# The inverse norms of q and k in a windowed attention layer: Newton steps on GpSimd replaced by a logarithm and an exponential on ScalarE

## What is computed

```python
def l2norm(t):
    return t / jnp.maximum(jnp.linalg.norm(t, axis=-1, keepdims=True), 1e-12)
...
def attn_layer(x, Wqkv, qs, ksc, Wo):
    q, k, v = jnp.split(x @ Wqkv, 3, -1)          # 16 heads of 64
    ...
    q = l2norm(q) * qs
    k = l2norm(k) * ksc
    q = q * cos * scale + rotate_half(q) * sin * scale
    k = k * cos * inv + rotate_half(k) * sin * inv
    out = local_attention(q, k, v)                # windows of 32, softmax
    return out.transpose(0, 2, 1, 3).reshape(b, n, INNER) @ Wo
...
for i in range(6):
    x = attn_layer(shift_tokens(x), Wqkv[i], q_scale[i], k_scale[i], Wo[i]) + x
    x = ffn_layer(shift_tokens(x), ...) + x
```

## Time and profile before

| | |
|---|---|
| median of 3 runs | 5080.17 us (5074.98 to 5081.27) |
| profiled execution | span 5070.2 us from the first to the last instruction |
| PE matmul busy | 4363.6 us (86%) |
| PE weight load busy | 3053.5 us (60%) |
| DVE busy | 3369.4 us (66%) |
| ACT busy | 2462.3 us (49%) |
| POOL busy | 2562.9 us (51%) |
| mean granted clock of TensorE | 0.949 of full speed |

### The profile page before, as it was taken

One profiled execution on the slowest core, in us unless ns is written; L12 is line 12 of the kernel. 1 busy time (PEld: TensorE's weight loads), 2 busy tenths in 40 slices (PEclk: granted clock), 3 DMA queues, 4 the chain that ended last, 5 costly groups with the idle time before them and its releaser, 6 DMA issues. The chain is left out here.

```text
span 5070.2 us, 182187 instructions
## 1 busy us (share of the span) xinstructions
PE 4363.6 (86%) x69459; PEld 3053.5 (60%) x69459; DVE 3369.4 (66%) x7024; ACT 2462.3 (49%) x5161; POOL 2562.9 (51%) x4541
## 2 busy tenths in 40 slices
PE   8999956866899988998789988899888998799986
PEld 5777733654566655666566665666656666466663
DVE  3555533266777757777577775777757776677765
ACT  3555543222555535555355553555535555355542
POOL 0000000011787717877177872778627776278761
PEclk9999967988999999999999998999999999999998
DMA  1000001201222212222122221222212222122211
GB/s 37 5 4 4 2 1 40 70 7 41 71 65 68 57 30 66 65 65 57 37 61 65 67 53 39 65 65 65 50 39 65 65 65 50 45 61 66 65 47 34
DMA packets 453969, 243.92 MB, mean 48 GB/s; under 512 B 41158, under 2 KB 447892, under 8 KB 452116
## 3 DMA queue, kind: packets, MB, share of 16 engines
q1 hardware_dynamic: 453140, 232.66, 18.6%
HBM read 35.40 MB, written 4.19 MB: 8 GB/s over the span
## 5 line engine op out<-in xcount | busy, mean ns | idle before, releaser
L2453 DVE TENSOR_TENSOR n_tt<-n_pp,n_rot 128x1024 f32<-128x1024 f32 x768 | 922.4, 1221 | 528.9 <-ACT n_sq L2316 528.1
L1949 POOL TENSOR_TENSOR n_pre<-n_tt 128x512 f32<-128x512 f32 x768 | 961.2, 1275 | 233.1 <-DVE n_tt L2453 232.4
L2065 PE MATMUL n_pp<-n_wqkv,n_xT 128*128 128x512 f32 x1536 | 793.9, 619 | 11.1 <-ACT n_xT L2311 10.1
L1984 POOL TENSOR_TENSOR n_pre<-n_pre,n_rn 128x512 f32<-128x512 f32 x768 | 776.9, 1043 | 34.5 <-POOL n_rn L1972 34.5
L2316 ACT ACTIVATE n_sq<-n_pp 128x512 f32<-128x512 f32 x768 | 459.0, 598 | 594.0 <-PE n_pp L2065 583.4
L2081 PE MATMUL n_pp<-ident,n_pre 128*128 128x128 f32 x3072 | 452.8, 282 | 152.8 <-POOL n_pre L1984 152.6
L2328 ACT COPY n_qkT<-n_pp 128x512 f32<-128x512 f32 x768 | 437.3, 594 | 290.1 <-PE n_pp L2081 288.7
L2081 PEld LDWEIGHTS n_pp<-ident,n_pre 128*128 128x128 f32 x3072 | 366.3, 146 | 292.9 <-issue 287.8
L2460 DVE TENSOR_REDUCE n_ss<-n_sq 128x8 f32<-128x512 f32 x768 | 519.3, 676 | 0.0
L2095 PE MATMUL n_pp<-n_wo,n_OT 128*128 128x128 f32 x3072 | 403.4, 286 | 57.5 <-ACT n_OT L2334 57.5
L2095 PEld LDWEIGHTS n_pp<-n_wo,n_OT 128*128 128x128 f32 x3072 | 366.6, 196 | 102.1 <-ACT n_OT L2334 101.4
(11 more groups left out here) (263 smaller groups left out, 8187.8 us busy)
## 6 DMA issues: line engine op xcount, KB each, us to landing
n_V<-n_Vn SPq DMA_DIRECT2D x768, 128.0 KB, 2.6
n_Vx<-n_Vn SPq DMA_DIRECT2D x384, 128.0 KB, 2.5
n_Vx<-n_Vn SPq DMA_DIRECT2D x576, 64.0 KB, 2.2
n_wqkv<-in_L_ffn_Wqkv SPq DMA_DIRECT2D x6, 1536.0 KB, 6.8
e_w<-in_L_ffn_w SPq DMA_DIRECT2D x32, 256.0 KB, 3.0
m_Y<-e_ye SPq DMA_DIRECT2D x64, 64.0 KB, 2.0
n_wo<-in_L_ffn_Wo SPq DMA_DIRECT2D x6, 512.0 KB, 7.3
a_xs<-in_L_attn_x SPq DMA_DIRECT2D x16, 128.0 KB, 2.1
```

The costliest lines, as they stand in the source:

```text
L1949: nc.gpsimd.tensor_tensor(d, s[0], s[1][:, :, ::-1, :], ALU.add).then_inc(s_add, 1)
L1984: nc.gpsimd.tensor_tensor(d, d, bcast(rn[:, j, t, 8 * half:8 * half + 8], 2, D), ALU.mult).then_inc(s_kn, 1)
L2065: nc.tensor.matmul(pp[:, c % 2, :], xT[:, j * P:(j + 1) * P], wqkv[:, t * I + 512 * half:t * I + 512 * half + 512], start=True, stop=True) ...
L2453: nc.vector.tensor_tensor(tt[:, c % 4, :, :].rearrange("p s (h d) -> p s h d", d=D), bcast(pp[:, c % 2, :].rearrange("p (h d) -> p h d", d ...
```

## The change

GpSimd keeps the clamp of the sums of squares, now `clamp_squares`, and the products. A new function of ACT, `inverse_norms`, takes the natural logarithm of the clamped sums into a new tile `lg` and then the exponential of minus a half times it into `rn`. The products wait for `s_rn`, which ACT now raises. At the start of each layer ACT asks for the table set that has both functions. In the prologue of a layer ACT makes the pair ahead of the square of chunk 5; in the attention it makes it behind the first two squares of each half, for the second half of N at j = 0 and for the first half of N + 1 at j = 1.

```diff
-            def inverse_norms(N, j):
+            def clamp_squares(N, j):
 
                 x = ss[:, j, :, :].rearrange("p t h -> p (t h)")
-                y = rn[:, j, :, :].rearrange("p t h -> p (t h)")
-                steps = Steps(pool, s_nd, NORM_STEPS)
...
                 after(pool, s_ss, 8 * N + 4 * j + 4)
-                after(pool, s_kn, 8 * N - 4 + 4 * j)
                 held(pool, s_held)
-                link(nc.gpsimd.tensor_scalar(x, x, 1e-24, None, ALU.max))
...
+                nc.gpsimd.tensor_scalar(x, x, 1e-24, None, ALU.max).then_inc(s_clamp, 1)
 
             def norm(N, j, r):
                 t, half = 1 - r // 2, r % 2
+                after(pool, s_rn, 2 * N + j + 1)
                 after(pool, s_add, 8 * N + 4 * j + r + 1)
...
+            def inverse_norms(N, j):
+
+                after(act, s_clamp, 2 * N + j + 1)
+                nc.scalar.activation(lg[:, j, :, :], ss[:, j, :, :], ACT.Ln).then_inc(s_ln, 1)
+                after(act, s_kn, 8 * N - 4 + 4 * j)
+                after(act, s_ln, 2 * N + j + 1)
+                nc.scalar.activation(rn[:, j, :, :], lg[:, j, :, :], ACT.Exp, scale=-0.5).then_inc(s_rn, 1)
...
             def prologue(N, l):
+                nc.scalar.preload_act_table_set("natural_log_exp_and_others")
                 for kind, c in PROLOGUE:
                     bank = bank_of[kind, c]
+                    if (kind, c) == ("qk", 5):
+                        inverse_norms(N, 0)
...
                     if nxt:
                         square(N + 1, 4 * j)
                         square(N + 1, 4 * j + 1)
+                    if nxt or not j:
+                        inverse_norms(N + j, 1 - j)
+                    if nxt:
                         copy_v(N + 1, 1 - u, 2 * j, bank("v", 2 * j, 1), pairs[0] + u)
```

More of the change, by code:

```diff
@@ L1684, in l1_network @@
     TG = GR * NT
-    NORM_STEPS = 13
     ident, X, neghalf = env["ident"], env["X"], env["neghalf"]
@@ L1760, in l1_network @@
         rn = sb("rn", [P, NT, 2, H])
-        nt = sb("nt", [P, 2 * H])
+        lg = sb("lg", [P, NT, 2, H])
         pre = sb("pre", [P, NT, 2, I])
@@ L1806, in l1_network @@
         s_rn = sem("norms_made")
-        s_nd = sem("norm_steps")
+        s_clamp = sem("squares_clamped")
+        s_ln = sem("norms_logged")
         s_kn = sem("qk_normed")
@@ L1992, in prologue @@
                     add(N, c)
-                inverse_norms(N, 0)
+                clamp_squares(N, 0)
                 for r in range(4):
@@ L2003, in attention @@
                     stage(N + 2, u, b + 2)
-                inverse_norms(N, 1)
+                clamp_squares(N, 1)
                 for r in range(4):
@@ L2009, in attention @@
                         add(N + 1, c)
-                    inverse_norms(N + 1, 0)
+                    clamp_squares(N + 1, 0)
                     for r in range(4):
```

## The result

The changed kernel takes 4911.6 us (median of 4 runs, 4901.34 to 4916.32); the kernel before, run beside it on the same chip, takes 5077.7 us (4 runs, 5074.98 to 5081.27). The ratio is 0.9676, interval 0.9664 to 0.9688. The mechanism is as forecast and its size is not. What remains to be explained is why the gain is larger than the sum: the forecast added the printed waits of PE at five places of a layer, and those in its middle gave more than was printed.

A forecast was written before the change was run, and what follows sets the result against it. PE's waits for GpSimd's products with the inverse norm, 152.6 us, were taken as what the change could free. Five places gave 19.65 us a layer, 118 in six, plus 17 for the clock: 5080.2 - 135 = 4945 us, range 4918 to 4990.

The forecast's parts named there:

- the step from span to median: The 10.0 us between the profiled span of 5070.2 and the median of 5080.2 us, taken over as it stands.
- (d): Middle of a layer: all 8.9 us of PE's printed waits for the products go.
- (e): Last sequence of a layer: PE's wait of 1.8 us for the products goes.
- (a): Prologue of a layer: with a round trip of 1.06 us, PE's wait of 7.44 us shrinks by 4.65 to 2.8.
- (b): First sequence, first half: the exponentials are next late, so PE gains 2.9 us, not 4.67.
- (c): First sequence, second half: the exponentials are next late, so PE gains 1.4 us, not 2.59.
- (f): PE's granted clock behind the three long waits: 2.9 us a layer regained, 17 us in all.
- Only the edges gain: Rival, 10%: the middle's freed wait reappears at ACT's copies; only 54 us gained, 5026 us.
- ACT's queue becomes the bound: Rival, 4%: ACT stands at the logarithm, delaying everything behind it; at 3.5 us a call, 5264 us.
- The tables do not stay loaded: Rival, 2%: logarithm and exponential each fetch their own table in every call; 5215 us.

The follow-up runs named there:

- pad13: The changed kernel with thirteen dummy steps on GpSimd between clamp and products, making a call about as long as before; 5069.5 us, ratio 0.9991.
- pad7: The changed kernel with seven linked dummy steps on GpSimd between clamp and products; 4934.2 us, ratio 0.9714.
- newton2: The kernel before the change with two Newton steps instead of three; 4944.7 us, ratio 0.9752.
- `middle`: The change only in the sequences between the first and last of each layer, Newton steps on GpSimd elsewhere; 5003.0 us, ratio 0.9854.
- the repetition: The changed kernel run once more, unaltered, in a later call; 4915.5 us, ratio 0.9684 against the kernel before.
- `tables`: The changed kernel with a table load forced ahead of the logarithm and of the exponential in each call; 5120.7 us, ratio 1.0096.

## Why the prediction was right in its mechanism, and where its size was wrong

**The mechanism held.** GpSimd's calls are one clamp and a wait of 1.44 us (0.7 to 2 forecast), its busy time fell by 598 us (600), the wait for `n_pre` is 14.3 us (under 25), and the exponentials wait 2.17 and 0.79 us in the first sequence (2 and 1). The kernel pad13 shows that this call's length is all that the gain hangs on. The time came out 6.4 us below the range, and two steps of the sum put it there, the price of the waits in the middle and the step from span to median; with either of them right the time would have been inside.

**The middle (d): the term that was mis-sized.** "All 8.9 us" was right in kind: pad7 and newton2 get it back whole, `middle` alone gives 71.7 us. In size it was 12.45 us a layer, 21 us more in six. The step that failed was to take the printed idle time for the price of a wait. Behind the output projection each printed wait cost 0.16 us more, in all 114 waits of the middle, so that the waits alone are 11.77 us a layer where 8.9 were taken, 17 us more in six; the rest is within what two executions differ by. The last sequence (e) gave 2.39 us for 1.8, or 1.54 by the repetition: no difference that the runs can tell.

**The prologue (a): the trip was sized too long.** It is 0.67 us, not 1.06, since the three handovers cost 0.03, 0.09 and 0.09 us instead of 0.2 each; GpSimd's 0.18 was the wrong model for handovers that involve ScalarE. The wait that is left is 2.39 us for 2.8. Together with a part of the clock for which I had taken nothing, the place gave 5.55 us for 4.65.

**The first sequence (b), (c): right, in its sum by luck.** The exponentials are next late, as named. The waits fell from 4.67 to 2.17 and from 2.59 to 0.79, by 2.5 and 1.8 us where 2.9 and 1.4 were forecast; the sum of 4.3 us agrees because the two errors cancel.

**The clock (f): about the right sum, from parts of which one was left out.** As the prediction did, I take the length of a window times what its clock lacks to full speed as lost. Before, that was 2.5, 2.4 and 1.7 us; now it is 5.2 x 0.33 = 1.7, 5.6 x 0.30 = 1.7 and 0. Regained are 0.8 us in the prologue (nothing was taken), 0.7 in the first half (1.2 was taken) and 1.7 in the second (1.7 was taken). That is 3.3 us for 2.9, and an estimate only, since the windows do not hold the same work. With the first sequence's share of it, 4.3 + 2.4 = 6.7 us stand against 6.68 measured.

**The step from span to median.** The 10.0 us taken over from before were not time around the span: every timed execution on record after it has 1.75 to 1.85 us between its span and its time. So the profiled execution before took about 5072 us, and the median of 5080.2 lay some 8 us above it, within the spread of that kernel's executions (5067.3 to 5081.7 us in the later calls). Its medians there were 5074.7, 5071.7 and 5072.9 us, so the 5080.2 of the start lay at the high end. The gain, each time against the kernel before on the same chip, came out as 166 and 157 us; the spans' 158.6 lies between. Of the 33.6 us by which the forecast was too high, 10 are this step and 23.6 the terms above (158.6 by the spans against 135), of which the middle has 21.

**The rivals.** *Only the edges gain* falls with `middle`. *ACT's queue becomes the bound* falls here: the slack ahead of the output copy is still 1.47 us, and PE's waits for the output copies are 57.9 us for 57.5 before. That ScalarE's queue does bind once a call lasts some 3 us is shown by `tables`. *The tables do not stay loaded* falls, since the activations carry no load, and its cost was measured at the other end: 5120.7 us, less than the 5215 that I gave, because a base of 4912 and not 4945 stood under it and the kernel lost 1.16 us a call, not 1.5.

The range failed for a reason that its bounds could have held: all of the clock and short trips were in it, but (d) was bounded only from below, by waits that return, and never from above by what a printed wait leaves out.

## What to carry to other kernels

In this kernel a chain of small dependent steps on an engine that paces others cost its length and nothing else. It paid to shorten the call until the engine had slack: 30% of the links gave back about four fifths of the gain, and in the middle of a layer a still shorter call gave nothing more. When waits of a pipelined engine are priced, compare the distance of the starts with and without the wait in the same program. Here the printed idle time was too little by the same 0.16 us in each of 114 waits behind one kind of instruction, while the removal of 84 waits at another place gave about what was printed, so the surplus has to be read for each place. And do not take the difference between a median and one profiled execution's span for time around the span: here it was 1.8 us, and the other 8 us were spread between executions.

## What the runs showed of the hardware that I had not expected

- The handovers that involve ScalarE are short: 0.03 us from GpSimd's clamp in the 12 calls in which ScalarE stood waiting for it, 0.09 us from the logarithm to the exponential and 0.08 to 0.09 us to GpSimd's product in all 192, against 0.18 us between GpSimd's last Newton step and its product.
- A small activation can be recorded as starting before the one ahead of it ends: the exponential ends at 2471.63 in the prologue, while the next square is recorded from 2471.54. With such overlaps on both sides of the pair, ScalarE's busy time rose by 50 us for 87 us of new instructions.
- In 378 of the 384 forced loads of `tables` the activation followed its load of 1283 ns at 0.01 us (the other six waited for the clamp), and each load began within 0.02 us of the end of the instruction before it.
- The granted clock was 0.67 and 0.70 in the windows behind waits of 2.01 and 2.17 us, and 1.00 behind one of 0.79 us.
